# Cross attention on one core: nine preparation steps spread over ten key tiles, and the key copies sent out in the next slot

## What is computed

```python
q = heads(xn @ Wq + bq)                 # 16 heads of 8
k, v = heads(ctx @ Wk + bk), heads(ctx @ Wv + bv)
attn = softmax(q @ k.T * 8 ** -0.5)     # 100 x 1444 for each head and batch
x = x + (attn @ v) @ Wo + bo
```

## Time and profile before

| | us |
|---|---|
| median of 3 runs (lowest, highest) | 6484.08 (6472.69, 6489.01) |
| the profiled execution, its own time | 6483.54 |
| its span, first to last instruction | 6481.7 |
| busy: PE, DVE, ACT, POOL | 5180.3, 4109.6, 2978.3, 1581.1 |
| one slot of cross attention in L0; in L1 and L3 | 40.36; 38.41 |

### The profile page before, as it was taken

How to read it: one execution, slowest core, us unless ns; L and a number is a source line. 1 busy time by engine, 2 the same in 40 slices (tenths; PEclk the granted TensorE clock), 3 DMA queues, 4 the chain that set the end, 5 groups by cost and what they waited for, 6 DMA issues and landing times. The chain is left out here.

```text
span 6481.7 us, 151169 instructions
## 1 busy us (share of the span) xinstructions
PE 5180.3 (80%) x63886; PEld 3345.2 (52%) x63886; DVE 4109.6 (63%) x7852; ACT 2978.3 (46%) x4342; POOL 1581.1 (24%) x869
## 2 busy tenths in 40 slices
PE   3737999999964739999999857879575599999996
PEld 2614555555642615666666525555353266666663
DVE  5546888888855527777777643234445477777774
ACT  2223666666642214666666522212222266666663
POOL 2024444444312022222332110000301222233221
PEclk6557999999986558999999877779755699999997
DMA  3315555555402325555555211110141455555540
GB/s 73 86 40 166 161 161 160 162 160 160 146 7 62 86 79 159 166 173 175 164 160 167 65 27 46 48 40 1 41 84 44 138 168 169 176 165 161 172 135 15
DMA packets 558269, 740.34 MB, mean 114 GB/s; under 512 B 194586, under 2 KB 467770, under 8 KB 545210
## 3 DMA queue, kind: packets, MB, share of 16 engines
q1 hardware_dynamic: 557594, 730.67, 38.2%
HBM read 450.42 MB, written 278.22 MB: 112 GB/s over the span
## 5 line engine op out<-in xcount | busy, mean ns | idle before, releaser
L1210 DVE TENSOR_REDUCE maxima<-ps 100x1 f32<-100x482 f32 (+1 forms) x4608 | 2719.3, 649 | 898.1 <-PE ps L1055 888.1
L1165 ACT ACTIVATE probs<-ps 128x800 f32<-128x800 f32 (+1 forms) x2304 | 1800.4, 835 | 656.1 <-PE ps L1076 654.3
L1055 PE MATMUL ps<-kst,qst 48*100 48x482 bf16 (+1 forms) x4608 | 1117.3, 410 | 108.9 <-DMA qst<-cross_q_parts 52.4
L1262 POOL TENSOR_TENSOR kparts<-kf,zero 128x1444 bf16<-128x1444 f32 x192 | 498.1, 2594 | 2281.2 <-ACT kf L1137 2251.1
L1093 PE MATMUL ps<-probs,vals 128*9 128x100 f32 x36864 | 1012.5, 250 | 7.8 <-ACT probs L1165 0.8
L1076 PE MATMUL ps<-qst,kst 128*128 128x200 bf16 (+1 forms) x9216 | 999.4, 250 | 11.0 <-DMA qst<-nparts 4.6
L1076 PEld LDWEIGHTS ps<-qst,kst 128*128 128x128 bf16 (+1 forms) x9216 | 758.8, 98 | 250.9 <-issue 123.7
L1093 PEld LDWEIGHTS ps<-probs,vals 128*9 128x9 f32 x36864 | 734.3, 90 | 259.6 <-issue 219.2
L1055 PEld LDWEIGHTS ps<-kst,qst 48*100 48x100 bf16 x4608 | 341.9, 119 | 631.8 <-DVE maxima L1210 330.4
L1143 ACT ACTIVATE vals<-ps 128x512 f32<-128x512 f32 (+1 forms) x288 | 161.9, 562 | 466.5 <-PE ps L1038 466.5
L1027 PE MATMUL ps<-ident,ctok 128*128 128x128 f32 (+1 forms) x1152 | 195.0, 291 | 216.3 <-DMA ctok<-in_ctx_dram 112.2
(11 more groups left out here) (252 smaller groups left out, 5407.6 us busy)
## 6 DMA issues: line engine op xcount, KB each, us to landing
kst<-ctx_k_stack SPq DMA_DIRECT2D x96, 2888.0 KB
ctx_k_stack<-kparts SPq DMA_DIRECT2D x192, 541.5 KB
ctx_k_stack<-kparts SPq DMA_DIRECT2D x192, 361.0 KB
ctok<-in_ctx_dram SPq DMA_DIRECT2D x96, 704.0 KB
ctx_k_stack<-kparts SPq DMA_DIRECT2D x192, 180.5 KB
c<-in_ctx_dram SPq DMA_DIRECT2D x32, 704.0 KB
o_self_sums<-osb SPq DMA_DIRECT2D x24, 800.0 KB
o_sums<-osb SPq DMA_DIRECT2D x96, 200.0 KB
```

The costliest lines, as they stand in the source:

```text
L1055: nc.tensor.matmul(ps[0:N, at:at + w], g.qst[s][row0:row0 + CROWS, j, N * e:N * e + N], g.kst[s][row0:row0 + CROWS, j, a:a + w], start=Tru ...
L1165: nc.scalar.activation(probs[kt % 2][hf][0:kts[kt], :].rearrange("p (k n) -> p k n", k=2), src, ACT.Exp).then_inc(exp_done, 1)
L1210: nc.vector.reduce_max(maxima[:, col:col + 1], ps[0:N, at:at + widths[c]], AX.X).then_inc(m_read, 1)
L1262: return nc.gpsimd.tensor_tensor(out, src, g.zero[0:src.shape[0], 0:1].to_broadcast(list(src.shape)), ALU.add)
```

## The change

The table `PREPS` gets one piece for each of the key tiles 0 to 7 and 9, so that K2 stands behind key tile 9 and no longer behind key tile 5. The standard deviation of the normalised context (L0 only) moves from key tile 10 to key tile 6, and its two VectorE steps with it. On POOL the normalisation goes ahead of the split of the keys. On SP, a slot now issues the context load, then the output of b - 1, and then the writes of the key copies of b + 2 directly ahead of the load of the same batch's stack; before, the copies of b + 3 were written at the end of the slot, and the stack was loaded at the start of the next.

```diff
--- before.py
+++ after.py
@@ -935,7 +935,8 @@
     KW = 16 * 2 * len(K_RUNS)
     Q_SLOTS = ((0, 3), (3, 2), (5, 1))
 
-    PREPS = {1: ("V0", "V1"), 2: ("V2", "T0"), 3: ("T1", "T2"), 4: ("K0",), 5: ("K1", "K2")}
+    PREPS = {0: ("V0",), 1: ("V1",), 2: ("V2",), 3: ("T0",), 4: ("T1",), 5: ("T2",), 6: ("K0",), 7: ("K1",), 9: ("K2",)}
+    STD_KT = 6
     PREP_INDEX = {"T0": 0, "T1": 1, "T2": 2, "K0": 3, "K1": 4, "K2": 5, "V0": 6, "V1": 7, "V2": 8}
     ring_of = lambda kt: ([4 * kt, 4 * kt + 1, 4 * kt + 2, 4 * kt + 3] + (["turn"] if kt == TURN_KT else [])
                           + list(PREPS.get(kt, ())))
@@ -1172,7 +1173,7 @@
                     act_exp(k, 2 * kt + 1)
                 for name in PREPS.get(kt, ()):
                     act_prep(slot, name)
-                if kt == KT - 2 and normed and k4 is not None:
+                if kt == STD_KT and normed and k4 is not None:
                     act_ctx_std(k4)
 
 
@@ -1251,9 +1252,9 @@
                 if normed and k4 is not None:
                     if 4 <= x < 4 + KT:
                         dve_stats(k4, x - 4)
-                    if x == MT - 8:
+                    if x == 4 * STD_KT - 4:
                         dve_aggregate(k4)
-                    if x == MT - 3:
+                    if x == 4 * STD_KT + 4:
                         dve_ctx_rstd(k4)
 
 
@@ -1292,10 +1293,10 @@
 
         def pool_slot(slot):
             k3, k4 = slot.k(3), slot.k(4)
+            if normed and k4 is not None:
+                pool_norm(k4)
             if k3 is not None:
                 pool_split_keys(k3)
-            if normed and k4 is not None:
-                pool_norm(k4)
 
 
         def sp_load_ctx(k):
@@ -1351,16 +1352,15 @@
                              src[a, :, HD:HD + 1, :].to_broadcast([4, HD, N])).then_inc(o_moved[s], 16)
 
         def sp_slot(slot):
-            if slot.k(2) is not None:
-                sp_stacks(slot.k(2))
             if slot.k(5) is not None:
                 sp_load_ctx(slot.k(5))
             if slot.k(-1) is not None:
                 sp_out(slot.k(-1))
+            if slot.k(2) is not None:
+                sp_keys_out(slot.k(2))
+                sp_stacks(slot.k(2))
             if slot.k(1) is not None:
                 sp_negmax(slot.k(1))
-            if slot.k(3) is not None:
-                sp_keys_out(slot.k(3))
 
 
         loops = (B - 5 - 1) // LAG
```

## The result

The changed kernel takes 7345.88 us (median of 4 runs, 7337.55 to 7349.04) against 6479.15 us for the kernel before (4 runs, 6472.69 to 6489.01): a ratio of 1.1334, 95% interval 1.1315 to 1.1354. The forecast was 7360 us. The profiled execution took 7346.47 us, 862.9 more than the profiled one of before.

What follows compares the result with a forecast made beforehand. PE bounds the kernel; the key-write and stack chain, hidden before, would now set slots of 48.8 us. L0's 245, L1 and L3's 603 and the first slots' 30 us add 878 to 6483.5: 7360 us, range 7050 to 7700.

Steps and rivals of the forecast that it cites:

- reads: On SyncE's queue: the eight reads back of the stored sums hold the queue for 5.1 us.
- key writes start: On SyncE's queue: key writes wait for the output's store, landing and reads, so they start 11.9 us into the slot.
- chain to x = 32: From the first key write through the stack load to the first maxima tile of batch b + 2: 23.3 us.
- tail at full clock: PE from x = 32 to the next slot's start: 10.3 us before, plus 0.8 for K2, so 11.1 us.
- slow clock: PE behind each wait: about 6.6 us at 1.2 GHz, costing 2.5 us a slot, ends 0 and twice that.
- The place of the wait, its length and its count: PE idle before the maxima line, 7 to 9 us once a slot, about 87 times, released by a DMA.
- The output's landing: On SyncE's queue: from storing the sums to the first read back, 3.3 us, with 4.8 as the upper end.
- Worth nothing in front of the wait: On PE: savings from the even spread and the moved standard deviation stall precede the 7.9 us wait and gain nothing.
- the rival "faster": At the wait of x = 32: the chain stays hidden, gaining at most 62 us, about 6420 us; chance 0.03.
- The key parts: POOL's split of the keys behind the later K2: ready 7.1 us into the slot, costing nothing behind the output.
- The first slots: At each layer's start: batch 1's keys wait for batch 0's x = 32 to 39; 10 us a layer, 30 us.
- The rival with the clock at full speed: PE behind the wait: full clock stays, slots of 46.3 us, 7146 us in total; chance 0.20.

Runs made afterwards that it cites:

- The queue alone: The kernel before with only SyncE's new order of the slot, pieces, standard deviation and POOL as before; 7298.16 us, beside 6485.14 for the kernel before.
- the spread alone: The changed kernel with SyncE's old queue order, so key writes stay at the end of the slot's list; 6947.02 us, 462 more than before.
- the output behind the stack: The changed kernel with the output of b - 1 moved behind the stack load in SyncE's list, K2 still in key tile 9; 6918.11 us.
- the standard deviation alone: The kernel before with only the standard deviation moved to key tile 6, its two VectorE steps with it; 6549.06 us, 1.0103 of before.

## Why the prediction was right

The total, 7360 against 7346, rests partly on two errors that cancel. Step by step, for a slot of L1 and L3:

| step | predicted, us | measured, us |
|---|---|---|
| sums copied, stored | 3.5 | 3.5 |
| stored to first read | 3.3 | 1.9 |
| reads | 5.1 | 5.2 |
| key writes start | 11.9 | 10.7 |
| chain to x = 32 | 23.3 | 23.8 |
| x = 32 | 35.2 | 34.5 |
| tail at full clock | 11.1 | 10.9 |
| slow clock | 2.5 | 3.2 |
| slot | 48.8 | 48.7 |

- **The place of the wait, its length and its count** are those forecast: in front of x = 32, 6.9 us in L1 and L3 (7.9 forecast), once in each of 87 slots. The queue alone reproduces nearly the whole loss.
- **The output's landing was mis-sized.** The 3.3 us came from a store issued directly behind the twelve query loads, with the DMA engines 0.90 busy in the 3 us before it. In the new list nothing is issued for 7.6 us before it, the engines' share is 0.00 in the last 3 us, and it takes 6433.02 - 6431.11 = 1.9 us; no slot has more than 2.1. The lower bound should have gone below the best row, since every row of before had traffic beside it.
- **The clock was mis-sized the other way**: 3.2 us (14.1 - 10.9). The clock came back after 9.2 us in the slot shown, and after 8.8 on average, not after 6.6 as behind L0. That row was also not a start from rest, as the forecast read it: PE had been at work for 9.0 of the 31.4 us before it, at a mean granted clock of 0.71. By the Trainium skill ("TensorE: Matmul & The Clock Gate", "HAM oscillation — how this bites in real kernels") half of the slow time is lost, 4.6 us for 9.2. In that slot the tail took 6427.57 - 6413.22 = 14.4 us, 3.4 more than at full clock, so that page's figure is too high here. One reason is in the rows: ahead of the turn (L1066) PE waits 0.84 us for VectorE, whatever the clock is. The page's main statement, that a DMA wait in each round throttles PE anew each round, is what the trace shows, in 87 of 87 slots.
- **K2** was costed at 0.8 us at full clock; taking it out of the tail, mostly at half clock, gave 0.9 to 1.0.
- **"Worth nothing in front of the wait"** holds. In L0 PE is ready for x = 32 at 30.4 us, 3.1 later than the 27.3 forecast (27.6 in L1 and L3), and its slots are no longer; only its hole is shorter, 4.1 us. But I took the moved standard deviation for harmless or a gain (the rival "faster" priced it at 62 us to the good). Its move costs 68 us when made alone. The full change hides that in the hole.
- **The key parts** were forecast at 7.1 us and hidden behind the output. They are ready at about 6.5 to 7 us, which the spread alone and the output behind the stack both show.
- **The first slots**: added up slot by slot, the 29 of each layer are longer by 245, 293 and 303 us, 842 of the 863 us. That leaves some 21 us for the rest, where 30 were estimated.

The rival with the clock at full speed is measured too: the slots of L1 and L3 that kept the clock take 45.3 us, 1.0 less than its 46.3, because x = 32 came at 34.3 and not 35.2. That the total is off by only 14 us is luck in part: the landing and the first slots were set too high, the clock too low.

## What to carry to other kernels

In an in-order DMA queue, add up what stands ahead of each transfer from the event that starts the queue's list, and compare the end of the chain with its first use; a start-up stretch in which the consumer does wait gives the length of a chain that is hidden everywhere else. If a hole opens on PE, add the slow clock behind it; here that held for holes of 3 us as for those of 7. And before evening out work, check that anything waits for it: here the spread itself was worth nothing that could be measured, and what travelled with it (a later last key piece, a table load in the middle of the slot) cost time.

## What was not expected of the hardware

- With the full change the tail is as long behind L0's holes (4.1 us on average) as behind those of L1 and L3 (6.9): 14.1 us, where 10.9 is the full-clock value. With the output behind the stack, holes of 3.2 us gave 13.4.
- The clock was also lost without any long hole: in the kernel with the standard deviation alone PE's longest wait in a slot was 1.46 us, and of 27 slots with equal waits 16 lost the clock and 11 kept it. What decides between them is not shown here.
- In all 87 slots of the change a store of 200 KB to DRAM, issued while the DMA engines were idle, had landed within 1.9 to 2.1 us (that is when the first read back is issued). In the 87 slots of before, with other traffic, it took 3.3 to 5.9 us.
